# Grouped-query attention stage: another order of TensorE's output, score and sum matmuls

## The reference, cut to what matters

```python
q = (query @ Wq).reshape(b, t, h, d)          # h = 32 heads, d = 128
k = (key @ Wk).reshape(b, t, kv_h, d)         # kv_h = 8
v = (value @ Wv).reshape(b, t, kv_h, d)
q = apply_rope(q)
k = apply_rope(k)
q = q.reshape(b, t, kv_h, g, d)               # g = 4 query heads share a key head
logits = jnp.einsum('btkgd,bTkd->bkgtT', q, k) * ATTN_MULT
logits = MAX_ATTN_VAL * jnp.tanh(logits / MAX_ATTN_VAL)
logits = jnp.where(m, logits, -1e+30)
weights = jax.nn.softmax(logits, axis=-1)
attn = jnp.einsum('bkgtT,bTkd->btkgd', weights, v)
return attn.reshape(b, t, h * d) @ Wo
```

## Time and profile before

| | |
|---|---|
| median of three timed runs | 3298.14 us |
| profiled execution | 3307.61 us |
| its span, first to last instruction | 3305.8 us |
| PE busy | 3086.6 us (93%) |
| DVE busy | 2092.0 us (63%) |
| POOL busy | 1851.0 us (56%) |
| ACT busy | 1237.8 us (37%) |
| mean granted TensorE clock | 0.964 |

### The profile page before, as it was taken

How to read it: one execution, slowest core, us unless ns; L and a number is a source line. 1 busy time by engine, 2 the same in 40 slices (tenths; PEclk the granted TensorE clock), 3 DMA queues, 4 the chain that set the end, 5 groups by cost and what they waited for, 6 DMA issues and landing times. The chain is left out here.

```text
span 3305.8 us, 41113 instructions
## 1 busy us (share of the span) xinstructions
PE 3086.6 (93%) x14547; PEld 2478.6 (75%) x14547; DVE 2092.0 (63%) x2607; ACT 1237.8 (37%) x1898; POOL 1851.0 (56%) x1243
## 2 busy tenths in 40 slices
PE   7999679999999995899999999999999999998799
PEld 6888558788788774677777777777777787776677
DVE  3232257777777752667666767767776677675575
ACT  3111155555555531433333333433343434332322
POOL 4232255444454433666676767676767776664343
PEclk9999889999999997899999999999999999999699
DMA  7333501111101103222233222332223332321321
GB/s 199 110 126 112 176 26 39 65 45 52 64 33 65 52 32 132 94 101 102 89 127 140 102 95 95 121 146 95 95 95 109 121 138 91 118 100 53 143 71 51
DMA packets 171548, 315.66 MB, mean 95 GB/s; under 512 B 10360, under 2 KB 86776, under 8 KB 171432
## 3 DMA queue, kind: packets, MB, share of 16 engines
q1 hardware_dynamic: 171432, 314.17, 27.3%
HBM read 247.03 MB, written 67.11 MB: 95 GB/s over the span
## 5 line engine op out<-in xcount | busy, mean ns | idle before, releaser
L1783 DVE RECIPROCAL g_rsum<-gp_sum 128x512 f32<-128x512 f32 x128 | 429.1, 3352 | 58.1 <-PE gp_sum L1873 58.1
L1841 PE MATMUL gp_p<-g_xn_hi,g_wq_hi 128*128 128x512 f32 x1024 | 404.3, 395 | 28.5 <-POOL g_wq_lo L1529 28.5
L1841 PE MATMUL gp_p<-g_xn_lo,g_wq_hi 128*128 128x512 f32 x1024 | 403.3, 394 | 0.0
L1841 PE MATMUL gp_p<-g_xn_hi,g_wq_lo 128*128 128x512 f32 x1024 | 402.7, 393 | 0.0
L1897 PE MATMUL gp_y<-g_wo_hi,g_at_hi 128*128 128x512 f32 x992 | 389.4, 392 | 1.0
L1897 PE MATMUL gp_y<-g_wo_hi,g_at_lo 128*128 128x512 f32 x992 | 386.5, 390 | 0.0
L1897 PE MATMUL gp_y<-g_wo_lo,g_at_hi 128*128 128x512 f32 x992 | 386.5, 390 | 0.0
L1529 POOL TENSOR_TENSOR g_wq_lo<-g_wq_raw,g_wq_hi 128x1024 fp32r<-128x1024 f32 x130 | 310.4, 2410 | 1.6 <-ACT g_wq_hi L1627 1.6
L1529 POOL TENSOR_TENSOR g_at_lo<-g_at_raw,g_at_hi 128x512 fp32r<-128x512 f32 x128 | 179.8, 1404 | 217.1 <-ACT g_at_hi L1627 217.1
L1627 ACT ACTIVATE g_q_hi<-g_q_raw 128x512 fp32r<-128x512 f32 x128 | 81.2, 634 | 537.3 <-POOL g_q_raw L1560 537.3
L1744 DVE TENSOR_TENSOR g_q_raw<-gp_p,g_cos_q 128x512 f32<-128x512 f32 x128 | 88.6, 692 | 293.7 <-PE gp_p L1841 254.9
(11 more groups left out here) (255 smaller groups left out, 7341.5 us busy)
## 6 DMA issues: line engine op xcount, KB each, us to landing
g_wq_raw<-in_L_Wq SPq DMA_DIRECT2D x64, 1024.0 KB, 7.4
g_wo_raw<-in_L_Wo SPq DMA_DIRECT2D x62, 1024.0 KB, 6.4
values_split<-c_v SPq DMA_DIRECT2D x64, 256.0 KB, 2.8
keys_split<-c_k SPq DMA_DIRECT2D x32, 512.0 KB, 2.7
g_k<-keys_split SPq DMA_DIRECT2D x32, 512.0 KB, 3.3
g_v<-values_split SPq DMA_DIRECT2D x32, 512.0 KB, 7.7
c_cx_raw<-in_ctxT SPq DMA_DIRECT2D x16, 512.0 KB, 7.4
a_x<-in_x SPq DMA_DIRECT2D x16, 512.0 KB, 4.5
```

The source lines that it names most:

```text
L1783: V.reciprocal(rsum[:, :], p_sum[:, :]).then_inc(rsum_done, 1)
L1841: mm = M(bank[:, :], w[a][:, i, cols], x[b][:, i, :], start=(i == 0 and t == 0), stop=(i == KT - 1 and t == 2))
```

## The change

Only the order of calls in `attend` (L1902) changes; each call issues the same instructions as before. One of four heads of output unit 2 goes ahead of scores(0); the rest of it and two heads of unit 3 go ahead of scores(2); the rest of unit 3 and all of unit 4 stand between values(0) and scores(3); unit 5 alone and half of unit 6 stand between values(1) and values(2). For n = 0, where `first` is set, `out` issues nothing.

```diff
                 out(0)
                 out(1)
+                out(2, range(0, 1))
                 scores(n, 0)
                 scores(n, 1)
-                out(2)
+                out(2, range(1, G))
+                out(3, range(0, 2))
                 scores(n, 2)
                 values(n, 0)
-                out(3)
-                out(4, range(0, 2))
+                out(3, range(2, G))
+                out(4)
                 scores(n, 3)
                 values(n, 1)
-                out(4, range(2, G))
                 out(5)
-                out(6, range(0, 1))
+                out(6, range(0, 2))
                 values(n, 2)
-                out(6, range(1, G))
+                out(6, range(2, G))
                 out(7)
                 values(n, 3)
```

## The result

The changed kernel takes 3317.07 us (median of five, 3311.19 to 3318.37), the kernel before 3299.82: ratio 1.0052 (1.0038 to 1.0066). It is slower by 17 us; I had forecast +10 and 3308.1, with a range up to 3316. The direction and the mechanism were right; the size was too small, and the time lies 1 us over the range.

What follows compares the result with a forecast made beforehand. The prediction took DVE's chain from sum(1) to add(4) as TensorE's pace up to out(6). Its terms, 30 x 0.30 + 0.95 = +10.0 us on the 3298.14 median, gave 3308.1 us, range 3299 to 3316.

Steps and rivals of the forecast that it cites:

- What bounds the step: Inner step: from sum(1) to out(6) TensorE goes at DVE's pace, through reciprocal(1), normalise and add(4).
- Part 1: Head 0 of unit 2 ahead of scores(0): scores(0) starts as before, path cost 0, 0.68 us of work banked.
- Part 2: Outputs ahead of scores(2): out(3) stops for add(1), values(0)'s products start later, path cost +0.30 us a step.
- Parts 3 and 4: From sum(0) on: sum(1) moves +0.30; out(6) waits 1.64 us for add(4) where 0.19 was; projection +0.30.
- Part 5: Last step: three later matmuls reach reciprocal(2) and the tail, about 0.95 instead of 0.30; group ends +0.30.
- The sum: All steps together: 30 x 0.30 + 0.95 = +10.0 us, giving 3317.6 profiled and 3308.1 on the timed scale.
- The term 30 x 0.30: Thirty grouped-query steps, each priced at +0.30 us, excluding the last step.
- the forecast's own base, 3298.14: Median of three timed runs of the kernel before, 9.5 us lower than the profiled execution.
- The upper bound of 3316: Top of the range: a costlier stop at out(3), +0.57 us a step, gives +18, taken to 3316.
- A: Rival: filled gaps are a gain, DVE isn't the pace; 1.3 us a step, -41 us, 3257; chance 0.06.
- B: Rival: out(3) doesn't stop or add(1) comes in time; -0.07 a step, -2 us, 3296, no difference; chance 0.15.
- C: Rival: the clock falls in the new 1.6 us stop; +56 us, 3364 with the +10; chance 0.03.

Runs made afterwards that it cites:

- Experiment 3: Kernel before with only the later edits (unit 4 whole ahead of scores(3), unit 5 and half of unit 6 ahead of values(2)): 3341.06 us, ratio 1.0126.
- experiment 5: Changed kernel with add(4) ahead of reciprocal(1) on DVE: 3294.45 us beside 3301.39 for the kernel before, ratio 0.9981.
- experiment 6: Changed kernel up to values(0), with the kernel before's order behind it: 3291.36 us beside 3301.39 for the kernel before, ratio 0.9975.
- experiment 2: Kernel before with only head 0 of output unit 2 moved ahead of scores(0): 3299.93 us beside 3300.82, ratio 0.9995.
- Experiment 4: Changed kernel with add(1) ahead of mask(0) on DVE: 3299.86 us beside 3300.82 for the kernel before, ratio 0.9997.
- experiment 8: Changed kernel with add(1) ahead of mask(0), add(4) ahead of reciprocal(1), add(5) ahead of mask(3) on DVE: 3263.1 us, ratio 0.9884 to kernel before.
- experiment 1: Kernel before run again with no edit: 3304.0 us beside 3300.82, ratio 1.0006.
- experiment 9: Kernel before with add(1) ahead of mask(0), add(4) ahead of reciprocal(1), add(5) ahead of mask(3) on DVE: 3326.61 us, ratio 1.0072.

## Why the prediction was right or wrong, point by point

- **What bounds the step.** Right. DVE's chain from sum(1) to add(4) paces out(6) and the projection behind it. Experiment 3 shows it with 1.37 us in and 1.39 out, and experiment 5 by taking add(4) off the chain. It holds while reciprocal(1) waits for sum(1); experiment 6 shows the other side. A slip that nothing rests on: the two waits together, 56.8 us of some 1740, are 3% of the stage, not 2.
- **Part 1, no gain ahead of scores(0).** Right: scores(0) stays where the projection puts it (6.57 us behind the first output matmul in both kernels), its stop shrinks to 0.69 start to start, and experiment 2 measures the edit alone at nothing.
- **Part 2, the stop at out(3).** Right in place and nearly in size: forecast +0.30 at values(0), 0.33 in the step shown, 0.34 on average. (Before, unit 3 started at 2028.89, so 3.3 us later than its new place and not two; add(1) was over long before.) Experiment 4 takes it away and the 0.40 us a step are gone.
- **Parts 3 and 4.** Right: out(6) starts 0.06 behind add(4), 1.54 us late; forecast 17.32 behind scores(0), measured 17.34. But I took every matmul behind the first one after a stop at c, and the 34 behind out(6) at an unchanged 7.89 us. In the step shown they took 7.98 (2045.03 to 2053.01): starts right behind the stop lie 0.23 to 0.24 apart where c is 0.2265. Averaged over the 27 steps, the delay against before is 0.34 us at values(0), 0.36 at out(6) and 0.40 at the projection (7.94 us for the 34 matmuls, 7.90 before). What spreads those starts I did not test.
- **Part 5.** Right: last step +0.97 (forecast 0.95), group ends +0.3 each. The runs bear out the source of the latter: the group ends keep their +0.3 in experiment 6, which has only the front part, and lose it in experiment 3, which has only the later one, and in experiment 4, which takes away the stop at out(3).
- **The sum: the step that failed.** The term 30 x 0.30 was mis-sized. An inner step costs 0.40 us and not 0.30, 27 x 0.10 = 2.7 us in all, for the reason under parts 3 and 4, so 10.0 forecast stands against 12.7 and 13.5 in the stage. On the forecast's own base, 3298.14, that gives 3311 to 3312, inside the range. The other 5 to 6 us up to 3317.07 have no term in the prediction: 1.7 of them are the base, which five runs put at 3299.82, and some 4 lie outside the stage's measured cost, their cause open. The upper bound of 3316 priced a costlier stop at out(3) and nothing for the scatter of whole executions, which lay between 3294.56 and 3307.33 for the kernel before, where I had three within 2 us to go by.
- **Rivals.** A (a gain) is refuted by the stop at out(6), which holds TensorE until add(4) ends, and for the head ahead of scores(0) by experiment 2. What A wanted came only once DVE's order was changed too: experiment 8 is 38 us faster than before, where A had 41; that the two sizes are so near is chance, since A had TensorE's order do it alone. The Trainium skill's page Perfetto Trace Analysis (Optimization Strategy) says to make what a gap waits for start sooner; experiments 5 and 8 did that and gained. B (no stop at out(3)) did not happen, but experiment 4 made it happen and showed its price, 3299.86: no difference. C (the clock) did not happen: the granted clock is 1.00 through the inner steps (1740 to 2160 us, for one) with the 1.5 us stop in each, and its mean between the stage's first projection and its tail is 0.99 in both kernels. The Trainium skill's page TensorE: Matmul & The Clock Gate (Part 1: The HAM clock gate) says that the gate halves the clock unless recent activity holds it open; inside the groups, stops of 1.5 us had no such end.

## What to carry to other kernels

Work put ahead of a wait is worth something only if the thing after the wait doesn't start later for it; count, for each instruction that feeds a slower engine's queue, how many matmuls stand in front of it before and after. When two engines pass buffers to and fro, change both orders together: here the new TensorE order alone costs 0.5%, the new DVE order alone costs 0.7%, and the two gain 1.2%. And look at the weight loads' waits too, since a short stop hides in the matmuls' modelled ends. Last, an instruction that comes earlier on its engine need not end earlier: look at what runs beside it.

## What the runs showed of the hardware that I had not expected

- DVE's mask(3) has two SBUF inputs and takes 1.3 to 2.8 us instead of 0.69 in an inner step where it starts while POOL works through g_wq_lo, and then it ends about 0.55 us behind POOL's instruction, however early it starts. Before, in one inner step (POOL's two g_wq_lo end at 2040.60, the mask at 2041.14):

```profile
2035.85 4.75 POOL L1529 TENSOR_TENSOR g_wq_lo<-g_wq_raw,g_wq_hi 128x1024 fp32r<-128x1024 f32 x2
2039.00 2.14 DVE L1777 TENSOR_TENSOR g_prob_raw<-g_prob_raw,g_keep 128x512 f32<-128x512 f32 x1
```

  In experiment 3 the mask starts later and takes 1.31 us, in experiment 5 earlier and takes 2.76, in experiment 9 it starts behind POOL's end and takes 0.68. An add, with one PSUM and one SBUF input, put in front of it (experiment 8) takes its usual 0.74 in the same stretch. The Trainium skill's page SBUF — State Buffer (Who interferes with whom) says that a DVE instruction with two SBUF inputs contends with a GpSimd instruction that reads SBUF, and that one with at most one SBUF input, outside the 2-port modes, does not; these rows agree.
- The changed stage repeats to about 1 us between profiles (1650.8 and 1651.1 before, 1663.6 and 1664.6 changed), while single executions of one kernel lie up to 13 us apart. Part of that lies behind the stage, where the longer stretches are those with the lower granted clock (experiment 1).
